# Graph attention layer on one core: products with the probabilities stationary, and one score tile of ten made by ScalarE and GpSimd

## The reference

```python
for h in range(Ws.shape[0]):
    Wx = x @ Ws[h] + Wb[h]
    d = Wx.shape[-1]
    s = Wx[v_tgt] @ a_w[h, :d] + Wx[v_src] @ a_w[h, d:] + a_b[h]
    s = jax.nn.leaky_relu(s, negative_slope=0.2)
    alpha = _segment_softmax(s, v_tgt, n)
    outs.append(jax.ops.segment_sum(alpha[:, None] * Wx[v_src], v_tgt, num_segments=n))
return jnp.stack(outs, axis=1).reshape(n, -1)
```

## Time and profile before

| | us |
|---|---|
| runs | 2269.34, 2272.47, 2274.48 (median 2272.47) |
| the profiled execution | 2274.44 |
| its span | 2272.7 |
| last layer, steps: first scores to the end of the last weighing | 1992.1 to 2254.9 |
| one head, scores of tile 0 to the next tile 0 (heads 0 and 1; heads 2 to 5) | 33.0; 34.0 |

### The profile page before, as it was taken

How to read it: one execution, slowest core, us unless ns; L and a number is a source line. 1 busy time by engine, 2 the same in 40 slices (tenths; PEclk the granted TensorE clock), 3 DMA queues, 4 the chain that set the end, 5 groups by cost and what they waited for, 6 DMA issues and landing times. The chain is left out here.

```text
span 2272.7 us, 39837 instructions
## 1 busy us (share of the span) xinstructions
PE 2066.5 (91%) x15006; PEld 1608.6 (71%) x15006; DVE 1573.7 (69%) x3095; ACT 957.0 (42%) x1444; POOL 665.8 (29%) x488
## 2 busy tenths in 40 slices
PE   5999979899899999899999899999898996978886
PEld 4899937788788888788888787888785554433332
DVE  6789754778764778764777765678855235699985
ACT  0222213666333666433666433666420023045444
POOL 0000015300554200554210554200350000088785
PEclk9999989999999999999999999999999997999998
DMA  2000041789711698811688812588963300000001
GB/s 75 24 25 36 32 143 60 133 143 154 157 47 52 120 151 144 171 44 55 112 150 149 177 34 65 99 147 148 205 153 90 68 12 22 0 1 1 0 1 46
DMA packets 490381, 195.82 MB, mean 86 GB/s; under 512 B 441767, under 2 KB 460199, under 8 KB 490195
## 3 DMA queue, kind: packets, MB, share of 16 engines
q1 hardware_dynamic: 490195, 193.31, 41.8%
HBM read 62.94 MB, written 25.45 MB: 39 GB/s over the span
## 5 line engine op out<-in xcount | busy, mean ns | idle before, releaser
L720 PE MATMUL psum<-turned_probability_parts,values_high 125*128 125x125 bf16 x1600 | 278.6, 221 | 49.9 <-DMA turned_probability_parts<-probability_parts 23.2
L922 DVE CUSTOM_DVE_ANT_0 probabilities<-psum,counts 125x1250 f32<-125x1250 f32 x160 | 233.5, 1460 | 114.9 <-PE psum L722 114.6
L1480 ACT ACTIVATE probabilities<-probabilities,row_peaks 125x1250 f32<-125x1250 f32 x160 | 214.5, 1341 | 176.2 <-DVE row_peaks L926 176.2
L722 PE MATMUL psum<-turned_probability_parts,values_low 125*128 125x125 bf16 x1600 | 277.8, 220 | 0.0
L721 PE MATMUL psum<-turned_probability_parts,values_high 125*128 125x125 bf16 x1600 | 277.6, 220 | 0.0
L1680 DVE SCALAR_TENSOR_TENSOR probability_parts<-probabilities,row_masses,probability_parts 125x1250 bf16<-125x1250 f32 x160 | 251.6, 1573 | 13.5 <-ACT probability_parts L1492 13.3
L2033 POOL TENSOR_TENSOR logs_and_shifts<-logs_by_source,target_shifts_spread 125x1250 f32<-125x1250 f32 x80 | 208.2, 2619 | 107.3 <-ACT target_shifts_spread L2190 67.9
L1492 ACT ACTIVATE probability_parts<-probabilities,row_masses 125x1250 bf16<-125x1250 f32 x160 | 214.1, 1338 | 46.4 <-DVE row_masses L934 43.1
L2307 PE MATMUL psum<-probabilities_turned,values_and_ones 125*65 125x512 f32 (+1 forms) x480 | 190.1, 540 | 23.5 <-ACT probabilities_turned L2208 13.1
L720 PEld LDWEIGHTS psum<-turned_probability_parts,values_high 125*128 125x128 bf16 x1600 | 158.0, 99 | 73.8 <-issue 67.9
L2307 PEld LDWEIGHTS psum<-probabilities_turned,values_and_ones 125*65 125x65 f32 x480 | 63.6, 142 | 136.2 <-issue 113.7
(11 more groups left out here) (335 smaller groups left out, 5061.0 us busy)
## 6 DMA issues: line engine op xcount, KB each, us to landing
weight_stage<-in_L_gnn_m_w SPq DMA_DIRECT2D x32, 256.0 KB, 2.9
block_inputs_kept<-nodes SPq DMA_DIRECT2D x8, 896.0 KB
counts_kept<-counts_by_target_rows SPq DMA_DIRECT2D x10, 625.0 KB, 3.1
logs_kept<-counts SPq DMA_DIRECT2D x1, 5468.8 KB
nodes<-block_inputs_kept SPq DMA_DIRECT2D x12, 448.0 KB
turned_probability_parts<-probability_parts SPq DMA_TRANSPOSE x320, 3.6
counts_by_target<-counts_kept SPq DMA_DIRECT2D x2, 2187.5 KB
logs_by_source<-logs_kept SPq DMA_DIRECT2D x1, 4375.0 KB
```

The lines of the kernel that those rows point to most:

```text
L720: pe.matmul(out, lh, rh, start=first, stop=False, skip_group_check=True)
L722: return pe.matmul(out, ll, rh, start=False, stop=last, skip_group_check=True)
L922: dve.tensor_tensor_reduce(prob[0:TILE, T % 2, :], scores, fx.count_src[0:TILE, i, 0:NODES], scale, MASKED, ALU.add, ALU.max, p[:, 0:1]).t ...
L1480: nc.scalar.activation(prob[0:TILE, T % 2, :], prob[0:TILE, T % 2, :], ACT.Exp, bias=fx.peak[0:TILE, T % 2, 1:2], accum_out=fx.mass[0:TILE ...
```

## The change

The weighing is turned round. Now a block of 125 targets of the probabilities is loaded (125 x 125), and the 65 columns of values move past it, for ten blocks, 20 passes a step. The result has targets on the partitions: five blocks of 65 columns fill a bank, a head takes two banks, and three (banks 0 to 2) are used in turn (rows_bank). The copy out of PSUM, the transposes back and the tile between are gone; VectorE divides straight from the bank, in steps j = 1 and 2 of the next head, after the last weighing of the head. The first product into a bank waits for the division of its last use.

Source tile 7 is scored without VectorE's long instruction. ScalarE makes max(target + lift, 0) from PSUM (lifted_scores, a Relu, issued ahead of the exponential of tile 6), GpSimd adds the offsets in place (in step j = 8, after the offsets of tile 8 and ahead of those of tile 9), and ScalarE's exponential has a bias of a fifth of the source's score. Two small VectorE instructions in the set-up make the two biases. Semaphore counts follow: lifts(T) is the number of such tiles before step T, scores(T) that of the others. The shift transpose no longer waits for the division.

The core of the diff:

```diff
+        lift = place("source_lifts", [128, HEADS3], F32)
+        calm = place("source_fifths", [128, HEADS3], F32)
...
-        weighted = packer(nc, LAST_AT)("weighted_values_turned", [128, 2, NODES], F32)
...
-        def back_bank(h, k):
-            return bank(6 if (h, k) == (HEADS3 - 1, 1) else 7)
+        def rows_bank(h, k):
+            return bank((2 * h + k) % 3)
...
+        LIFT = 7
+        def lifts(T):
+            return (T + TILES - 1 - LIFT) // TILES
+        def scores(T):
+            return T - lifts(T)
...
                 if j == 0:
                     pool.wait_ge(piece_copied, 4 * h + 4)
-                if T >= 2:
-                    pool.wait_ge(scored, T - 1)
+                if T >= 2 and (T - 2) % TILES == LIFT:
+                    pool.wait_ge(lifts_added, lifts(T - 1))
+                elif T >= 2:
+                    pool.wait_ge(scored, scores(T - 1))
                 nc.gpsimd.tensor_tensor(offset[0:TILE, T % 2, :], lw.logs[0:TILE, j, :], shifts[0:TILE, h % 2, :],
                                         ALU.add).then_inc(offset_ready, 1)
+                if j == LIFT + 1:
+                    n = lifts(T)
+                    pool.wait_ge(lifted, n)
+                    pool.wait_ge(offset_ready, T)
+                    at = prob[0:TILE, (T - 1) % 4, :]
+                    nc.gpsimd.tensor_tensor(at, at, offset[0:TILE, (T - 1) % 2, :], ALU.add).then_inc(lifts_added, 1)
...
+            dve.tensor_scalar(lift[0:TILE], column[0:TILE, LIFT, HEADS3:WAYS], BEND3, None, ALU.mult).then_inc(cols_ready, 1)
+            dve.tensor_scalar(calm[0:TILE], column[0:TILE, LIFT, HEADS3:WAYS], 0.2, None, ALU.mult).then_inc(cols_ready, 1)
...
             def out_part(h, k):
-                view = back_bank(h, k)[0:TILE, 0:HALF * WIDTH].rearrange("p (t d) -> p t d", d=WIDTH)
+                view = rows_bank(h, k)[0:TILE, 0:HALF * WIDTH].rearrange("p (t d) -> p t d", d=WIDTH)
                 m, v, n = mass[0:TILE, k, :], inverse[0:TILE, k, :], 2 * h + k
-                dve.wait_ge(back, n + 1)
+                dve.wait_ge(pv, TILES * (h + 1))
                 dve.tensor_scalar(m, view[:, :, HDIM3:WIDTH].rearrange("p t d -> p (t d)"), 1e-30, None, ALU.max).then_inc(part_own, 1)
                 dve.wait_ge(part_own, 2 * n + 1)
...
             for T in range(STEPS):
                 h, j = T // TILES, T % TILES
-                dve.wait_ge(offset_ready, T + 1)
-                if j == 0:
-                    dve.wait_ge(target_spread, h + 1)
-                if T >= 4:
-                    dve.wait_ge(pv, T - 3)
-                dve.scalar_tensor_tensor(prob[0:TILE, T % 4, :], region(3)[0:TILE], bend[0:TILE, j, h:h + 1],
-                                         offset[0:TILE, T % 2, :], ALU.max, ALU.add).then_inc(scored, 1)
+                if j != LIFT:
+                    dve.wait_ge(offset_ready, T + 1)
+                    if j == 0:
+                        dve.wait_ge(target_spread, h + 1)
+                    if T >= 4:
+                        dve.wait_ge(pv, T - 3)
+                    if j == LIFT + 1:
+                        dve.wait_ge(lifted, lifts(T))
+                    dve.scalar_tensor_tensor(prob[0:TILE, T % 4, :], region(3)[0:TILE], bend[0:TILE, j, h:h + 1],
+                                             offset[0:TILE, T % 2, :], ALU.max, ALU.add).then_inc(scored, 1)
                 if j == TILES - 6 and h < HEADS3 - 1:
                     shift_of(h + 1)
-                if h >= 1 and j in (3, 4):
-                    out_part(h - 1, j - 3)
+                if h >= 1 and j in (1, 2):
+                    out_part(h - 1, j - 1)
                 g, at = (T + AHEAD) // TILES + 1, (T + AHEAD) % TILES
                 if g < HEADS3:
...
-            dve.wait_ge(pv, STEPS)
-            a, z = CUTS[1]
-            dve.tensor_copy(weighted[0:WIDTH, (HEADS3 - 1) % 2, a:z], region(0)[0:WIDTH, a:z]).then_inc(last_copied, 1)
...
-            def copy_out(h):
-                act.wait_ge(pv, TILES * (h + 1))
-                if h >= 2:
-                    act.wait_ge(back, 2 * h - 2)
-                for a, z in ((0, NODES),) if h < HEADS3 - 1 else CUTS[0::2]:
-                    nc.scalar.activation(weighted[0:WIDTH, h % 2, a:z], region(0)[0:WIDTH, a:z], ACT.Copy).then_inc(out_copied, 1)
+            def lifted_scores(T):
+                h = T // TILES
+                act.wait_ge(scored, scores(T))
+                act.wait_ge(pv, T - 3)
+                nc.scalar.activation(prob[0:TILE, T % 4, :], region(3)[0:TILE], ACT.Relu, bias=lift[0:TILE, h:h + 1]).then_inc(lifted, 1)
             act.wait_ge(v_ready, TILES)
             for T in range(STEPS):
                 h, j = T // TILES, T % TILES
-                act.wait_ge(scored, T + 1)
+                if j == LIFT - 1:
+                    lifted_scores(T + 1)
+                if j == LIFT:
+                    act.wait_ge(lifts_added, lifts(T + 1))
+                    source = calm[0:TILE, h:h + 1]
+                else:
+                    act.wait_ge(scored, scores(T + 1))
+                    source = column[0:TILE, j, HEADS3 + h:HEADS3 + h + 1]
                 nc.scalar.activation(prob[0:TILE, T % 4, :], prob[0:TILE, T % 4, :], ACT.Exp,
-                                     bias=column[0:TILE, j, HEADS3 + h:HEADS3 + h + 1], scale=1.0 / UNIT3).then_inc(exped, 1)
-                if j == 0 and h >= 1:
-                    copy_out(h - 1)
+                                     bias=source, scale=1.0 / UNIT3).then_inc(exped, 1)
...
-            copy_out(HEADS3 - 1)
...
             def shift_turned(h):
                 if h == 0:
                     pe.wait_ge(cols_ready, 2)
-                elif h == 1:
-                    pe.wait_ge(piece_copied, 4)
                 else:
-                    pe.wait_ge(parted, 2 * h - 2)
+                    pe.wait_ge(piece_copied, 4 * h)
                 pe.wait_ge(shift_ready, h + 1)
                 pe.transpose(bank(7)[0:TILES, 0:TILE], shift[0:TILE, h % 2, :], fx.ident[0:TILE, 0:TILE]).then_inc(piece, 1)
...
-            def turn_back(h, k):
-                pe.wait_ge(out_copied, h + 1 if (h, k) != (HEADS3 - 1, 1) else HEADS3 + 1)
-                if h == HEADS3 - 1:
-                    pe.wait_ge(last_copied, 1)
-                    pe.wait_ge(peaked, PEAKS * HEADS3)
-                if k == 0:
-                    pe.wait_ge(piece_copied, 4 * min(h + 2, HEADS3))
-                elif h < HEADS3 - 1:
-                    pe.wait_ge(parted, 2 * h + 1)
-                for t in range(HALF):
-                    mm = pe.transpose(back_bank(h, k)[0:TILE, t * WIDTH:(t + 1) * WIDTH], weighted[0:WIDTH, h % 2, cols(k * HALF + t)],
-                                      fx.ident[0:WIDTH, 0:WIDTH])
-                mm.then_inc(back, 1)
             def weigh(T):
                 h, j = T // TILES, T % TILES
                 pe.wait_ge(exped, T + 1)
-                if j == 0 and h >= 1:
-                    pe.wait_ge(out_copied, h)
-                for a, z in CUTS:
-                    mm = pe.matmul(region(0)[0:WIDTH, a:z], values[0:TILE, j, h, :], prob[0:TILE, T % 4, a:z],
-                                   start=(j == 0), stop=(j == TILES - 1))
+                for t in range(TILES):
+                    k, at = t // HALF, (t % HALF) * WIDTH
+                    if j == 0 and t % HALF == 0 and 2 * h + k >= 3:
+                        pe.wait_ge(parted, 2 * h + k - 2)
+                    mm = pe.matmul(rows_bank(h, k)[0:TILE, at:at + WIDTH], prob[0:TILE, T % 4, cols(t)], values[0:TILE, j, h, :],
+                                   start=(j == 0 and t % HALF == 0), stop=(j == TILES - 1), skip_group_check=True)
...
-                if h >= 1 and j in (2, 3):
-                    turn_back(h - 1, j - 2)
...
-            for k in range(2):
-                turn_back(HEADS3 - 1, k)
```

More of the change, by code:

```diff
@@ L2262, in spread_targets @@
                 if h >= 1:
-                    pe.wait_ge(scored, TILES * h)
+                    pe.wait_ge(scored, scores(TILES * h))
                 for a, z in CUTS:
```

4 lines of the change are left out of this document (2 added, 2 removed).

## The result

The changed kernel takes 2411.3 us (median of 4 runs, 2407.38 to 2412.41) against 2272.7; the ratio is 1.0609, 95% interval 1.0590 to 1.0627. Its profiled execution took 2411.03 us, with a span of 2409.2 and a mean granted clock of 0.892, before 0.968. It is slower by 139 us where 5 us less had been forecast. The time is not in the forecast's own range (2262.5 to 2272.5) but where rival 1 had put it, 2403 (2386 to 2418): TensorE runs all steps of the layer at 1.2 GHz.

What follows compares the result with a forecast made beforehand. VectorE was taken to bound most of the last layer, TensorE's queue late head 6, GpSimd the last head. Terms -4.3 - 1.4 - 0.9 + 1.2 + 0.25 = -5.2 us gave 2267.3 us, own range 2262.5 to 2272.5.

Steps and rivals of the forecast that it cites:

- rival 1: TensorE stays at 1.2 GHz in the last layer and becomes the bound: 2403 us (2386 to 2418), chance 0.35.
- The weighing: TensorE, each step: 20 loads set the rhythm at 0.108 us each, 2.17 to 2.18 us, +0.08 a step, hidden.
- The rest of a head: TensorE's work besides the weighings if it stays at 1.2 GHz: 8.3 us in each of seven heads, 58 us.
- VectorE's wait for the turned-back output: VectorE's 0.72 us idle ahead of the division goes in each of heads 1 to 6: -4.3 us.
- Tile 7: Tile 7 scored without VectorE: +0.1 in heads 0 and 1, -0.5 in each of heads 2 to 5; about -1.4 us.
- the chain through GpSimd: Tile 6 to the next tile 0: offsets, addition, exponential, weighings and target scores end last, at 13.75 us.
- Last head: GpSimd sets the pace there, so its added addition costs +2.62 us.
- The end: After the last tile, copy and turning back go, -1.56 us; the last weighing adds +0.1.
- The set-up: Two small VectorE instructions ahead of the first peak cost +0.25 us.
- The weighing at full clock: TensorE's turned weighing at 2.4 GHz: loads of 125 columns come 0.108 us apart.
- Half-clock stretches: Heads 2 to 5: -0.5 each, taken half-way; head 1: +0.45 for a half chance; head 6: -0.65, half chance.
- Head 6: From tile 4, TensorE's queue: division wait -0.8, six weighings +0.5, half-clock stretch -0.65; sum -0.9 us.

Runs made afterwards that it cites:

- e2: Changed kernel with tile 7 scored by VectorE again, leaving only the turned weighing and the earlier division; 2412.4 us, ratio 1.0611.
- e5: Changed kernel with nine added products over 125 rows, 512 moving columns, result never read, ahead of the first weighing; 2413.0 us, ratio 1.0607.
- e4: Changed kernel with 102 columns of values, not 65, moved past each loaded block, the further 37 never read; 2313.9 us, ratio 1.0176.
- e6: Changed kernel with two heads' values (130 columns) moved past each loaded block, the second 65 never read; 2281.9 us, ratio 1.0043.
- e7: Changed kernel with 130 columns moved past each loaded block and tile 7 scored by VectorE again; 2308.9 us, ratio 1.0148.
- e8: e7 with TensorE weighing tile 3 ahead of the shift transpose; 2272.1 us, ratio 0.9994.
- e9: The kernel before with TensorE weighing tile 3 ahead of the shift transpose; 2270.1 us, ratio 0.9989.
- e11: e7 with TensorE weighing first in steps 4 to 7, ahead of the shift transpose and small shift products; 2265.3 us, ratio 0.9962.
- e12: The kernel before with TensorE weighing first in steps 4 to 7; 2278.1 us, ratio 1.0009.
- e3: Changed kernel with 36 added products of 48 rows and 512 moving columns, result never read, ahead of the first weighing; 2415.9 us, ratio 1.0628.

## Why the prediction was wrong

The step that failed is the one under the whole sum, in "The weighing": 0.108 us a load and 2.17 to 2.18 us a weighing, "hidden wherever VectorE or GpSimd sets the end". That holds at 2.4 GHz only. At 1.2 GHz the loads came 0.209 us apart, a weighing took 4.19 us, and TensorE set the pace of the whole layer. The question was seen, as rival 1, and given 0.35 against 0.38. The runs settle it: this stream did not bring the clock up from a cold start (the changed kernel, e2) and did not keep it from a warm one (e5), and the clock comes back as more columns move past each load (e4, e6). "Against: loads and passes follow each other without a gap" was the wrong reason to doubt it: TensorE was busy 290.00 of 290.00 us and stayed at 1.2 GHz. That later rows of before stand at 1.00 spoke of a stream of long passes, which the change removes. With no row for the new stream at either level, the nearest evidence was a layer that begins at 0.50 and falls five times more, and it spoke for rival 1. The prediction counted four: the stretch in head 6 is the fifth. It is 3.4 us long as the others (a clock of 0.92 over 21.92 us gives 3.5), not 1.3.

Rival 1's own working held. Forecast 0.208 us a load and 4.16 a weighing, measured 0.209 and 4.19. The rest of a head was put at 8.3 us and measured 51.09 - 10 x 4.19 = 9.2, which over seven heads is 6 of the 8 us by which 2403 lies under 2411.

The terms of the forecast, where the clock is up (e6, against before):

- VectorE's wait for the turned-back output: forecast -0.72 a head; in head 1, tile 0 to tile 6 takes 18.59 us instead of 19.39, **-0.80**. Right, and in heads 0 to 6 the division did not wait.
- Tile 7: forecast +0.1 in heads 0 and 1 by the chain through GpSimd, 13.75 us; measured **13.78** in head 1 and **14.23** in head 0, against 13.65 in e7 in both. The chain is right; the price is right in odd heads alone, since the median of 2.62 stood for two values of 2.40 and 2.85. In head 1 the offsets (2.40) and the addition (2.81) are off by 0.2 each way, which is luck. Scoring tile 7 elsewhere buys nothing here: that chain takes the place of VectorE's 1.43 us.
- Last head: forecast +2.62, measured **+2.9** (26.84 for 23.93); the addition took 2.84 us in the mean, near the upper bound.
- The end: forecast -1.56 + 0.1; from the scores of the last tile to output_masses before takes 6.85 us (2249.64 to 2256.49) and e7, where the clock is up, 5.38 (2286.11 to 2291.49), **-1.47**. Right. The set-up's +0.25 was not isolated.
- The weighing at full clock: forecast 0.108 us a load; measured 0.109 with 65 columns (e5) and with 102, and 0.111 with 130. Right.
- Half-clock stretches: the halves were guesses. e8, e9, e11 and e12 change nothing but the order of TensorE's queue, and the falls moved with it, in the heads before the last each up to 2.4 us behind a wait of 0.9 to 1.5 us; why one wait brings a fall and the next of the same length none stays open. That with turned weighing a fall can last longer (20.5 us in e7, 3.4 in heads 2 to 6 of before) was missing from the sum.
- Head 6: -0.9 was not isolated. e9 took 3.3 us out of it by TensorE's order alone.

The Trainium skill, page "TensorE: Matmul & The Clock Gate", section "LDWEIGHTS (loading the stationary operand)", gives a load as its columns over 1.2 GHz, with no clock level. For 125 columns that is 0.104 us, and agrees with the 0.108 at full clock; at half clock the loads came every 0.209, twice that. The measurement decides, and this is what turned a lost clock into 139 us.

## What to carry to other kernels

Before a product is turned round so that it is bound by its loads, ask what TensorE's clock will be under the new stream, and treat a stage that begins at 1.2 GHz, or falls there now and then, as one that may stay there: then loads cost double too. Columns that a pass can move under its load for nothing may be worth moving even if no one reads them (e6 took 129 us off the changed kernel, and stayed 0.4% above the kernel before). In TensorE's queue, put the ready long work ahead of small products that wait for another engine, and look again, since the wait may only move (e9, e12). And where an engine's durations fall into two groups, as GpSimd's did here, ask what tells the groups apart before taking the median.

## What had not been expected of the hardware

- Products with 48 rows and 512 moving columns, one pass each, kept TensorE busy without a gap, and the clock went from 1.00 to 0.50 while they ran (e3); with products of 125 rows and two passes each in the same place it stayed at 1.00 (e5). Which of the two differences did it was not tried.
- At 0.50 the stream with 65 columns a load stayed down for the rest of the layer, 390 of 390 us busy (2000 to 2390); with 102 columns the falls in the heads lasted 6.8 to 23.9 us, with 130 from 3.4 to 20.5.
- GpSimd's addition over 125x1250 takes 2.40 or 2.85 us by the numbers of the buffers, in each of 80 instructions of each run. The buffers lie at different addresses; what about the addresses does it was not tried. The addition of tile 7 is always of the slow kind (2.82 to 2.85 in e6).
- One order of the same instructions changed e12's single runs to between 2263 and 2285 us, a wider scatter than any other version's here. Why e6 and e7, which differ only in who scores tile 7, fell so differently (for 20.5 us once, and five times), with the same wait in both, stays open.
